# Moving two of four layout transfers behind the maxima, and the next batch's context loads behind the head stacks, in a gated cross-attention layer

## What is computed

```
x = x + tanh(g_xattn) * attention(layernorm(x), ctx, ctx, mask)     # 16 heads of 32, causal
x = x + tanh(g_ffn)  * channel_mix(layernorm(x))                    # r * ((relu(k)^2) @ Wv)
```

## Time and profile before

| | before |
|---|---|
| median of 3 runs | 1900.03 us (1894.64 to 1905.4) |
| the profiled execution | 1893.25 us |
| its span, first to last instruction | 1891.5 us |
| PE busy | 1833.8 us, 97% of the span |
| DVE, ACT, POOL busy | 1426.0, 1095.0, 1159.2 us |
| the 16 DMA engines, attention part | 5 to 7 tenths busy in most of the 40 slices |
| TensorE clock granted | 0.993 of full speed over the span |

### The profile page before, as it was taken

How to read it: one execution, slowest core, us unless ns; L and a number is a source line. 1 busy time by engine, 2 the same in 40 slices (tenths; PEclk the granted TensorE clock), 3 DMA queues, 4 the chain that set the end, 5 groups by cost and what they waited for, 6 DMA issues and landing times.

```text
span 1891.5 us, 35048 instructions
## 1 busy us (share of the span) xinstructions
PE 1833.8 (97%) x10688; PEld 1425.6 (75%) x10688; DVE 1426.0 (75%) x3792; ACT 1095.0 (58%) x2055; POOL 1159.2 (61%) x1833
## 2 busy tenths in 40 slices
PE   6899999999999999999999999999999999999999
PEld 5577777777777777777777777777678888888887
DVE  6777778687787868778687876867678787887864
ACT  4656556565565656556555655656575565656562
POOL 2777777777767777777777776776752323323231
PEclk9899999999999999999999999999899999999999
DMA  7556575655657556665665666566243535354431
GB/s 220 123 118 160 129 171 126 150 142 129 153 131 168 139 131 149 135 150 130 163 143 124 153 134 152 129 166 162 78 134 107 161 101 157 104 144 121 125 98 67
DMA packets 170699, 259.06 MB, mean 137 GB/s; under 512 B 25200, under 2 KB 54896, under 8 KB 169744
## 3 DMA queue, kind: packets, MB, share of 16 engines
q1 hardware_dynamic: 170512, 256.81, 55.1%
HBM read 92.06 MB, written 33.59 MB: 66 GB/s over the span
## 4 chain that ended last, share of the span: by engine, by line
PE 81%; DVE 5%; DMA 4%; SPq 4%; issue 2%; ACT 2%; POOL 1%; ACTq 0%; DVEq 0%
PE proj_ps L41 13%; PE proj_ps L42 13%; PE proj_ps L43 13%; PE score_ps L1511 8%; PE value_ps L1552 7%; PE prob_ps L1535 7%; DMA q_stack<-max_rows 3%; PE score_ps L41 3%; PE score_ps L42 3%; PE score_ps L43 3%; SPq L369 2%; PE sum_ps L1560 2%; PE sum_ps L42 1%; PE sum_ps L43 1%; PE sum_ps L41 1%
## 5 line engine op out<-in xcount | busy, mean ns | idle before, releaser
L1151 DVE CUSTOM_DVE_ANT_0 score_ps<-score_ps,causal 128x128 f32<-128x128 f32 (+3 forms) x1024 | 488.4, 504 | 253.0 <-PE score_ps L1511 252.3
L746 ACT ACTIVATE probs<-prob_ps 128x512 f32<-128x512 f32 (+1 forms) x768 | 395.9, 529 | 366.9 <-PE prob_ps L1535 189.3
L1511 PE MATMUL score_ps<-k_stack,q_stack 97*128 97x128 f32 (+3 forms) x1024 | 317.2, 351 | 3.5 <-DVE least L1151 3.3
L1535 PE MATMUL prob_ps<-q_stack,k_stack 100*128 100x512 f32 (+3 forms) x1024 | 283.7, 318 | 26.2 <-DMA q_stack<-max_rows 26.0
L608 POOL TENSOR_TENSOR kact<-square,kact 128x512 fp32r<-128x512 f32 x64 | 95.7, 1505 | 305.6 <-ACT kact L832 305.6
L540 POOL TENSOR_TENSOR prob_sum<-probs 128x384 f32<-128x384 f32 x256 | 262.3, 1025 | 0.0
L1511 PEld LDWEIGHTS score_ps<-k_stack,q_stack 97*128 97x128 f32 x1024 | 188.8, 189 | 76.8 <-issue 39.0
L1535 PEld LDWEIGHTS prob_ps<-q_stack,k_stack 100*128 100x128 f32 x1024 | 192.6, 191 | 50.4 <-DMA q_stack<-max_rows 30.7
L543 POOL TENSOR_TENSOR prob_sum<-prob_sum,probs 128x256 f32<-128x256 f32 x256 | 203.0, 793 | 37.3 <-POOL prob_sum L540 0.9
L529 POOL TENSOR_SCALAR_AFFINE_SELECT probs<-probs 128x256 f32<-128x256 f32 x256 | 112.0, 437 | 165.7 <-ACT probs L746 165.3
L533 POOL TENSOR_SCALAR_AFFINE_SELECT probs<-probs 128x256 f32<-128x256 f32 x256 | 105.4, 412 | 117.6 <-ACT probs L746 117.5
(11 more groups left out here) (185 smaller groups left out, 4693.6 us busy)
## 6 DMA issues: line engine op xcount, KB each, us to landing
k_stack<-staged SPq DMA_DIRECT2D x384, 128.0 KB
q_stack<-staged SPq DMA_DIRECT2D x384, 128.0 KB, 3.1
turning<-in_x SPq DMA_DIRECT2D x65, 256.0 KB, 4.4
res<-x SPq DMA_DIRECT2D x64, 256.0 KB, 3.7
out_x<-res SPq DMA_DIRECT2D x64, 256.0 KB, 5.3
x_io<-in_x SPq DMA_DIRECT2D x63, 256.0 KB, 5.4
x<-x_io SPq DMA_DIRECT2D x63, 256.0 KB, 3.2
xT_room_low<-turning SPq DMA_DIRECT2D x60, 256.0 KB, 4.3
```

The costliest lines, as they stand in the source:

```text
L746: nc.scalar.activation(probs[:, u % RING, lo:hi], prob_ps[(3 * u + c) % 2][:, 0:hi - lo], ACT.Exp, scale=SCALE).then_inc(exp_done, 1)
L1151: nc.vector.tensor_tensor_reduce(out=here, in0=here, in1=causal[:, LATE - P * t:S], scale=-1.0, scalar=3e38, op0=ALU.add, op1=ALU.min, acc ...
L1511: last = nc.tensor.matmul(here[:, at:at + P * (t + 1)], q_stack[n][0:MASK_ROW + 1, j, P * t:P * t + P], k_stack[n][0:MASK_ROW + 1, j, 0:P ...
L1535: last = nc.tensor.matmul(here[:, at:at + width], k_stack[n][0:ROWS, j, P * k:P * k + P], q_stack[n][0:ROWS, j, P * k:S], start=True, stop ...
```

## The change

Nothing is computed in another way and no instruction is added or removed; PE's order stays as it is. Moved are:

- on SP, the third and fourth move of turned x, from slot 9 (behind the q stacks of head 12) to slot 10, behind the DMA of the maxima of heads 8 and 9;
- on SP, in slot 11, the four loads of the next context, from ahead of the q and k stacks of head 14 to behind them;
- on ACT, the high part of x's quarter 2 from slot 10 to slot 11, of quarter 3 from `second` to `third` of slot 11, and the context's high parts 0 and 1 from slot 11 to `first` of slot 12, behind the copy of the maxima and ahead of the first exponent; those of 2 and 3 stay in `third` and `fourth` of slot 12;
- on DVE, the low part of x's quarter 2 from `second` to `third` of slot 11, and that of quarter 3 from there to `second` of slot 12.

```diff
--- before.py
+++ after.py
@@ -443,28 +443,25 @@
                         load_residual(b - 1, 2)
                 if has_prev and s == 8:
                     load_residual(b - 1, 2)
-                if has_next and s == 9:
-                    move_normalised(b + 1, 0)
-                    move_normalised(b + 1, 1)
+                if has_next and s in (9, 10):
+                    move_normalised(b + 1, 2 * (s - 9))
+                    move_normalised(b + 1, 2 * (s - 9) + 1)
                 if 0 <= b < B and s == 0:
                     load_x(b + 1)
                 if has_prev and s in (7, 8):
                     store_x1(b - 1, s - 7)
                 if has_prev and s in (12, 13):
                     store_x1(b - 1, s - 10)
-                if has_next and s == 11:
-                    for k in range(K):
-                        load_c(b + 1, k)
                 if i % HG == 1 and 0 <= i + 3 < N:
                     stack_q(i + 3)
-                if has_next and s == 9:
-                    move_normalised(b + 1, 2)
-                    move_normalised(b + 1, 3)
                 if i % HG == 2 and 0 <= i + 2 < N:
                     stack_k(i + 2)
                 if i % HG == 3 and 0 <= i + 3 < N:
                     stack_q(i + 3)
                     stack_k(i + 3)
+                if has_next and s == 11:
+                    for k in range(K):
+                        load_c(b + 1, k)
                 if i == N - 12:
                     load_ffn("k")
                 if i == N - 6:
@@ -849,6 +846,9 @@
                     high_part_attn(K * b)
                 if 2 <= i <= N and i % 2 == 0:
                     copy_maxima(i // 2 - 1)
+                if 0 <= b < B - 1 and s == 12:
+                    high_part_c(b + 1, 0)
+                    high_part_c(b + 1, 1)
 
             def second(i, b, s):
 
@@ -860,7 +860,7 @@
                 if has_next and b >= 0 and s == 10:
                     high_part_x(b + 1, 0)
                 if has_next and b >= 0 and s == 11:
-                    high_part_x(b + 1, 3)
+                    high_part_x(b + 1, 2)
                 if now and s == 5:
                     seed_deviations(b + 1)
                 if i == N + 2:
@@ -889,8 +889,10 @@
                     copy_v(b + 1, s - 14)
                 if has_next and b >= 0 and s == 10:
                     high_part_x(b + 1, 1)
-                if has_next and b >= 0 and s in (11, 12):
-                    high_part_c(b + 1, 2 * (s - 11))
+                if has_next and b >= 0 and s == 11:
+                    high_part_x(b + 1, 3)
+                if has_next and b >= 0 and s == 12:
+                    high_part_c(b + 1, 2)
                 if i % HG == 0 and 0 <= i - VALUES < N:
                     invert_sums((i - VALUES) // HG)
                 if i == N - 6:
@@ -913,10 +915,8 @@
                     high_part_k(b + 1, 0)
                 if i % HG == 1 and s != 9 and 0 <= i - VALUES < N:
                     high_part_attn((i - VALUES) // HG)
-                if has_next and b >= 0 and s == 10:
-                    high_part_x(b + 1, 2)
-                if has_next and b >= 0 and s in (11, 12):
-                    high_part_c(b + 1, 2 * (s - 11) + 1)
+                if has_next and b >= 0 and s == 12:
+                    high_part_c(b + 1, 3)
                 if now and s in (6, 7):
                     apply_layernorm(b + 1, 2 * (s - 6) + 1)
                 if i == 0:
@@ -1264,8 +1264,8 @@
                 if has_next and b >= 0 and s == 8:
                     for k in reversed(range(K)):
                         turn_normalised(b + 1, k)
-                if has_next and b >= 0 and s == 11:
-                    low_part_x(b + 1, 2)
+                if has_next and b >= 0 and s == 12:
+                    low_part_x(b + 1, 3)
                 if now and s == 12:
                     low_part_attn(K * b)
                 if i % HG == 1 and 0 <= i - VALUES < N:
@@ -1307,7 +1307,7 @@
                 if has_next and b >= 0 and s == 10:
                     low_part_x(b + 1, 0)
                 if has_next and b >= 0 and s == 11:
-                    low_part_x(b + 1, 3)
+                    low_part_x(b + 1, 2)
 
             def fourth(i, b, s):
 
```

## The result

| | before | after |
|---|---|---|
| median of 14 runs each, on the same chip | 1899.87 us (1892.87 to 1905.4) | 1907.62 us (1903.81 to 1910.54) |
| ratio, 95% interval | | 1.0046 [1.0034, 1.0057] |
| the profiled execution | 1893.25 us | 1909.12 us |
| its span, mean granted clock | 1891.5 us, 0.993 | 1907.4 us, 0.992 |

The changed kernel is 7.75 us slower, where 9 us less were forecast. The two profiled executions lie 15.9 us apart: that of before stood 6.6 under its median, that of after 1.5 above. The traces therefore tell where the time went, and the medians how much there is: about half of what the traces differ by.

The account below looks back on a forecast made before the run. PE, busy 97% of the span, was taken as the bound, so only its waits and clock could be won: 16.9 + 2.8 + 1.0 - 11.7 = 9.0 us off 1893.25 gives 1884.2, plus 6.8 gives 1891; range 1880 to 1905.

Parts of the forecast that it names:

- The wait in slot 11 goes: Head of slot 11: with the first maxima issued 1.40 us earlier, PE no longer waits for them in ordinary batches.
- The wait goes in the ordinary batches (1.30 each, 16.9 in all): Slot 11: PE wins its whole wait for the first maxima, 1.30 us in each of 13 batches.
- nothing else is ahead of PE there: Head of slot 11: no other hold-up than the first maxima, so the gain is bounded only by the wait.
- 19.7 us (16.9 and 2.8): Slot 11's gain: 16.9 us in 13 ordinary batches, 2.8 in the first batch and the one with 1.71.
- The loads: SP, slot 11: first load issued 3.7 us later, landing 3.0 after issue; slot 12's first exponent late by 1.2.
- Its return: Slot 13, third scores: the late exponent costs PE 0.9 us in each of 13 batches, 11.7 in all.
- The second maxima: Head of slot 13: issued at 497.9 instead of 498.20, there at 501.6, PE waits 0.3 us.
- a wait of 0.3. It does not add up with the 0.9: Slot 13: of the 0.3 us wait for maxima and the 0.9 lost at third scores, only the larger counts.
- The clock: After the batch with the 1.71 us wait: less time at 1.2 GHz, a gain of 1.0 us, between 0 and 1.7.
- B: Rival, slot 13's third scores: loads land late, 1.9 to 2.45 us a batch, 1904 to 1912 us; chance 0.15.
- C: Rival, head of slot 13: second maxima land behind the loads, PE waits 1.7 us, time 1902; chance 0.13.
- The last shift, of 6.8 us from the profiled execution to the median: Whole kernel: the shown median, 1900.03, is 6.8 us above the profiled execution, turning 1884.2 into the forecast 1891.

Follow-up runs that it names:

- e8: e7 with DVE's addition of the third output share moved from slot 10 into slot 11, behind its first two maxima; 1885.4 us.
- e4: The changed kernel with ACT's first two context casts reading a weight that is always there, so they don't wait for the loads; 1896.58 us.
- e5: The changed kernel with all four context casts on ACT reading a weight, so none waits for the loads; 1895.01 us.
- e6: The changed kernel with the context's loads between the q and the k stacks of slot 11; 1897.21 us.
- e7: e6 with the k stacks of head 14 moved to slot 12, behind the DMA of the second maxima; 1885.1 us.
- e1: The kernel before with only the moves of x's quarters and their casts changed; loads and casts of context as before; 1912.29 us.
- e11: e1 with the k stacks put behind the DMA of the second maxima in slot 12; 1889.94 us.
- e3: The changed kernel with the context's loads ahead of the stacks of slot 11 again, casts left where the change put them; 1918.83 us.

## Why the prediction was wrong

The forecast was 1891, the time 1907.62, outside the range. By its steps:

- **The wait in slot 11 goes: right.** The first maxima are issued 1.45 us earlier (1.40 forecast), and the first probabilities start 1.49 earlier in their slot. The first batch's 3.58 fell to 0.71, but PE then idles 0.55 for DVE and 3.12 at the head of slot 12, for which the trace names no releaser, and that batch takes 74.4 us where it took 74.6.
- **"The wait goes in the ordinary batches (1.30 each, 16.9 in all)", since "nothing else is ahead of PE there": this step failed.** Only 0.69 a batch reached the slot's end. DVE starts on the first two maxima of slot 11 10.74 us after the start of slot 9 in both kernels: its addition of the third output share stands ahead of them, and that starts 0.20 into the slot in both, released by PE's last matmul of this share. PE's third scores stand for these maxima for 0.6 of the 1.49, in 14 batches (8.5 us), and e8 shows the next wait behind that one, for the bank that the same addition frees. The prediction asked what is late behind the removed wait for slot 13, and not here. Its 19.7 us (16.9 and 2.8) became 14 x 0.69 = 9.7, and next to nothing in the first batch.
- **The loads: a size.** The first is issued 4.04 later (3.7 forecast), the four take 2.4 to issue in the mean and up to 3.33 (1.93 forecast), and the first cast starts 3.4 after the first issue in the mean and 4.15 in the sample (3.0 forecast). Slot 12's first exponent is late by 1.8, not 1.2.
- **Its return: most of it at other places.** It was to reach PE through the reciprocal, the correction and the third scores of slot 13. That chain runs late as told (the correction stands 3.98), but PE idles at its end only four times, 0.8 us in all (by the starts of these scores it holds PE for 0.2 a batch). It meets the late exponents sooner, since they free the banks that its probabilities write: at the last probabilities of slot 12 (5.7 us in 7 times) and at the first of slot 13 (3.2 in 8), the 8.9 us of the waits' row. e4 and e5 take all of that back. By e5 the landings cost 0.58 in slot 12 and 0.44 in slot 13: 1.0 a batch, against 0.9 forecast. The size was nearly right, and that is luck: the exponent was later than assumed and the path another.
- **The second maxima, "a wait of 0.3. It does not add up with the 0.9": this step failed too.** They were to go out 0.3 earlier than before and go out 0.37 later, 18.46 after slot 9's start against 18.09, by the later and longer issue of the loads; and PE comes for them sooner. With no landing to wait for (e5) slot 13 is 0.60 longer than before, 0.53 of it at its first probabilities. It adds up, since the two delays of PE stand at different places, one behind the other.
- **The clock: the sign.** In place of one stretch at 1.2 GHz in the attention part there are two; the first stands behind the waits of 0.81 and 1.66, with a granted clock of 0.89 in the ten microseconds shown above. A gain of 1.0 was forecast.

So 0.69 is won and 0.6 + 1.0 = 1.6 returned, where the prediction had 1.30 and 0.9. Of the rivals, B (the loads land late) came true in part. Of C the place came true, a wait for the second maxima at the head of slot 13, but not its reason: it had them land behind the loads, over 5 us after issue, and in e5 PE starts 3.5 after their issue in the mean (3.0 to 4.8 in the ten batches in which it stood for them), no more than the 3.69 of the first maxima before. Each cost less than its own price, and together they are the result; they had been priced as alternatives, with 0.15 and 0.13. The Trainium skill ("DMA: Bandwidth & Descriptors", section "Queues, rings and completion order") spoke against this place. The trace does not settle its rule: with the loads directly ahead the maxima took 4.80 in the sample batch, where 3.69 was assumed, but with the same order 3.41 in the same batch of e5. What makes one batch differ from the other is not shown.

The last shift, of 6.8 us from the profiled execution to the median, also hid something: the profile of before was one of its quicker executions, and the two medians differ by half of what the traces do. That batches of one execution differ so much (after's from 82.0 to 85.8 us) is not explained here.

## What to carry to other kernels

When a wait of PE is removed, ask what ends next within the same slot before counting the whole of it: here half stayed. A queue with one issuer is a budget of positions: rank its DMAs by how soon the waiting engine comes for each, and put the small one that PE needs ahead of the big ones that it needs later; one DMA of 8 KB put ahead of three stacks gave 12 us (e6 to e7) and 22 (e1 to e11). Two returned delays at different places of a chain add up.

## What was not expected of the hardware

- Issue is not of a fixed price. Four loads of 256 KB take 1.93 to 1.94 us on SP in an easy stretch and 3.33 in the sample batch, where two moves and nine stacks had gone out since the maxima without a pause. In five of after's 15 batches the four take over 2.8. What holds the issue back is not shown. Single issues of L360 reach 1.85 us:

```profile
L360 SPq DMA_DIRECT2D turning<-in_ctxT x56: 327/328/1852, 168.6 to 1251.6; - x56
...
DMA to landing us min/median/max: 2.7/3.9/5.8
```

(durations in ns, least, median and largest). Before, the largest was 1.08.

- Behind waits of 1.7 to 3.2 us the clock was often lower, so they cost more than themselves. In e1, after the wait of 3.23 that ended at 427.92, the granted clock is

```profile
420.00:430.00 10.00, 6.77 (x58) 4.87 (x51) 5.03 (x12) 4.81 (x11) 9.63 (x12) 0.84 0.70 168
430.00:440.00 10.00, 10.00 (x41) 8.25 (x41) 6.37 (x19) 4.20 (x8) 4.48 (x8) 0.82 0.19 40
```

0.84 and 0.82 in the two stretches, 2.4 GHz with a piece at 1.2 in each. Past the first batch, e1 has eight such stretches in the attention part and e3 seven, with a mean clock of 0.986 and 0.987; e5 and e7, whose longest waits are 1.5 and 1.1, have none, and 0.993 and 0.994. An estimate from these means: 0.007 of e1's 1921 us is 13 us, nearly half of the 29.6 by which its trace is longer than that of before. Its seven executions go the same way, from 1902.9 us at 0.993 to 1922.85 at 0.986.
